# Edge keys by a TensorE matmul per job into PSUM, in place of a round trip through DRAM

## The chip, the cores and the metric

One core of a Trainium2 chip runs the whole program. TensorE (PE in the profile) multiplies matrices and writes only to PSUM; VectorE (DVE), ScalarE (ACT) and GpSimd (POOL) do the rest; SyncE (SP) issues transfers. The metric is the device time of one execution in microseconds (us), median of three.

## The reference, cut to what matters

A layer of a graph transformer over 384 nodes of width 1024: a layer norm, a graph attention with a mask made from 12288 edges, a mixer beside it, and after both a feed-forward part with one of eight experts. The change touches only the making of the mask:

```python
def _build_mask(edge_index, edge_type, edge_type_weights, dtype):
    src, dst = (edge_index[0], edge_index[1])
    w = jax.nn.softplus(edge_type_weights)
    mask = jnp.full((N, N), -jnp.inf, dtype=dtype)
    mask = mask.at[src, dst].set(w[edge_type - 1])
...
q = x @ wq.T + bq
k = x @ wk.T + bk
v = x @ wv.T + bv
q2 = (q @ wiq.T + biq).reshape(N, H, D).transpose(1, 0, 2)
...
scores = jnp.einsum('hnd,hmd->hnm', q2, k2) * scale + mask[None]
attn = jax.nn.softmax(scores, axis=-1)
```

An edge has the key `src * 384 + dst`. Where the same pair occurs more than once, the last edge counts, so the kernel has to find, among 128 edges that it scatters together, those that a later one overrides.

## The kernel before, in words

All products are made in float32r with each operand split in a high and a low part: high by high, low by high, high by low. **Column jobs** (`column_job`, L1143 to L1157) make 128 output columns of a projection: 8 matmuls with `w_hi` and the high input, 8 with `w_hi` and the low input (both L1151), 8 with `w_lo` (L1156), each 128x384 into one PSUM bank. The first stage is `FIRST` = 32 of them: q, k, v and the inner q, 8 each, into banks 0, 1, 6 and 7 in turn (`A_BANKS`). Row blocks of 18 matmuls of 128x512 follow (L1161, banks 2 to 7), with one column job between them, and then eight pairs of heads: scores (L1242), transposes (L1252), the product with v (L1262), and four column jobs each. The output projections and the feed-forward part end the program.

Weights come in 512 KB transfers on SP's queue (`load_weights`, L321) into slots. ACT rounds a slot to `w_hi` (L463), DVE subtracts to get `w_lo` (L789). In the first stage both run three jobs ahead of PE (`DEPTH` = 3). ACT then writes the high part of a job's result (L523) and DVE the low part (L856), the latter only for the first 24 jobs.

**The edges** are handled beside this, three columns of 128 edges in each of the 32 jobs. DVE casts the ends of the edges (L799), makes the keys as rows `erow` of a 96x128 tile (L802), and POOL stores them in `key_dram` (L413). SP then loads, for each job, 384 keys spread over all 128 partitions into one of two halves of `key_row` (L342), behind three waits: for `key_out`, for `xt_done`, and for the job two before it (`where_ready`); each stands on SP's queue ahead of the load of a later job's weights. In `job(a)` of DVE the three scans of L841 compare the spread keys with the key of the edge in each partition (`ekey`, a column), under the triangle `tri`, and sum up the matches in `dup`; L848 makes the table address `where` from it. POOL scatters each column of edges into one of four tables in DRAM (L422), 96 scatters, and loads the tables back (L431). DVE merges them into `mask` (L864, L866) between the splits of the row blocks, ahead of the first scores.

The order on each engine is that of the program text; semaphores alone tie them. `where_ready` starts at 2 and goes up by one with each job's L848. `xt_done` tells that the input is split; `v_copied` and `score_read` stand ahead of the scores and of the second column job of a pair.

Of the kernel before, what the change touches and what calls it, by code (L numbers as in the profile page):

```python
# [15 lines left out]
F32 = mybir.dt.float32  # L16
F32R = mybir.dt.float32r
I32 = mybir.dt.int32
U32 = mybir.dt.uint32
ALU = mybir.AluOpType  # L20
# [4 lines left out]
P = 128  # L25
N = 384
D = 1024
NT = N // P
# [4 lines left out]
CH = E // P  # L33
CJ = 3
STEPS = CH // CJ
# [12 lines left out]
FIRST = 32  # L48
# [3 lines left out]
A_USES = [(A_SLOTS[a % 4], a // 4) for a in range(FIRST)]  # L52
# [39 lines left out]
LN_BANKS = ((6, 4, 2), (6, 4, 0))  # L92


C_ID, C_TRI, C_ONES, C_EIDX, C_ONE, C_ALL = 0, 128, 256, 384, 392, 520


def gps_layer(nc, x, out, weights, conv, down, upT, up_b, down_b, conv_b, disc, bias_cols,
              rows, edge_weights, edge_rows, edge_cols, consts):
    with ExitStack() as ctx:  # L100
# [3 lines left out]
        def sem(name):  # L104
            return ctx.enter_context(nc.semaphore(name))

        key_dram = nc.dram_tensor("key_dram", [CH, P], F32, kind="Internal").ap()
        tables = [nc.dram_tensor(f"table{g}", [N * N, 1], F32, kind="Internal").ap() for g in range(STREAMS)]


# [12 lines left out]
        U = sb("U", [P, 6 * D], F32)  # L123
        x_rows = U[:, 0:NT * D].rearrange("p (t d) -> p t d", t=NT)
        xn_rows = U[:, NT * D:2 * NT * D].rearrange("p (t d) -> p t d", t=NT)
        key_row = U[:, 3456:3456 + 2 * CJ * P].rearrange("p (s n) -> p s n", s=2)
        key_junk = U[:, 4224:4352]
        later = [U[:, g * NT * N:(g + 1) * NT * N].rearrange("p (t n) -> p t n", t=NT) for g in range(STREAMS - 1)]
        present = U[:, 4608:4608 + NT * N].rearrange("p (t n) -> p t n", t=NT)
# [11 lines left out]
        vs = sb("vs", [P, NT, 2, P], F32R)  # L141
# [3 lines left out]
        cst = sb("cst", [P, C_ALL], F32)  # L145
# [7 lines left out]
        ew_t = sb("ew_t", [P, 8], F32)  # L153

        v2f = V2[:].rearrange("p k n -> p (k n)")
        erow_i = v2f[0:CH, 0:2 * P].bitcast(I32)
        erow = v2f[0:CH, 2 * P:4 * P]
        ecol_i = v2f[:, 4 * P:4 * P + 3 * CH].bitcast(I32)
        v2_rows = v2f.rearrange("p (t d) -> p t d", t=NT)
        ecol = v2f[:, 1536:1536 + 3 * CH]  # L160
# [54 lines left out]
        ew_in = sem("ew_in")  # L215
        edges_in = sem("edges_in")
        x_in = [[sem(f"x_in{t}{c}") for c in range(2)] for t in range(NT)]
        key_out = sem("key_out")
        key_calc = sem("key_calc")
        key_in = [sem(f"key_in{s}") for s in range(2)]  # L220
        prep = sem("prep")
        aprep = sem("aprep")
        norm_step = sem("norm_step")
# [92 lines left out]
        @block.sync  # L316
        def _(sp):
            def load_weights(slot, use, src):

                sp.wait_ge(lo_ready[slot], use + 1)  # L320
                sp.dma_start(raw[slot][:], src).then_inc(w_in[slot], 16)  # L321

            for t in (0, 2):
                sp.dma_start(x_rows[:, t, 0:HALF], x[t * P:(t + 1) * P, 0:HALF]).then_inc(x_in[t][0], 16)
            load_weights(*A_USES[0], weights[0])
            sp.dma_start(ew[:], edge_weights.partition_broadcast(P)).then_inc(ew_in, 16)
            sp.dma_start(cst[:, C_TRI:C_ALL], consts[:, C_TRI:C_ALL]).then_inc(cst_in, 16)
            load_weights(*A_USES[1], weights[1])
            sp.dma_start(erow_i, edge_rows).then_inc(edges_in, 16)
            sp.dma_start(ecol_i, edge_cols).then_inc(edges_in, 16)  # L330
            sp.dma_start(bias[:], bias_cols).then_inc(const_in, 16)
            sp.dma_start(disc_in[:], disc).then_inc(const_in, 16)
            load_weights(*A_USES[2], weights[2])
            for a in range(3, FIRST + 2):
                if a < FIRST:
                    load_weights(*A_USES[a], weights[a])
                k, s = a - 3, (a - 3) % 2

                sp.wait_ge(key_out, 16)
                sp.wait_ge(xt_done, NT)  # L340
                sp.wait_ge(where_ready, k + 1)
                sp.dma_start(key_row[:, s, :],  # L342
                             key_dram[k * CJ:k * CJ + CJ, :].rearrange("c e -> (c e)").partition_broadcast(P)
                             ).then_inc(key_in[s], 16)
            sp.wait_ge(where_ready, FIRST)
            sp.dma_start(key_row[:, 1, :],
                         key_dram[(FIRST - 1) * CJ:FIRST * CJ, :].rearrange("c e -> (c e)").partition_broadcast(P)
                         ).then_inc(key_in[1], 16)
            for r in range(JOBS):
                load_weights(*slot_use(r), weights[32 + r])  # L350
            for b in range(16):
                load_weights(*C_USES[b], weights[72 + b])
                if b == 5:

                    sp.wait_ge(vs_ready, KB)
                if b == 7:

                    sp.wait_ge(score_read, KB * 6 + 1)
                if 5 <= b < 9:
                    load_weights(*E_USES[(b - 5)], weights[72 + 16 + (b - 5)])  # L360
            for e in range(4, 8):
                load_weights(*E_USES[e], weights[72 + 16 + e])

            sp.wait_ge(x2_turned, NT)
            sp.dma_start(bias_rows[0:1, :], rows[2:3, :]).then_inc(base_in, 16)

            sp.wait_ge(idx_ready, 1)
            expert = sp.value_load(pick_i[0:1, 0:1], min_val=0, max_val=EXPERTS - 1)
            sp.dma_start(raw_down, down[ds(expert, 1)].rearrange("a p k r -> (a p) k r")).then_inc(small_in, 16)
            sp.dma_start(raw_up, upT[ds(expert, 1)].rearrange("a p k r -> (a p) k r")).then_inc(small_in, 16)  # L370
            sp.dma_start(raw_upb, up_b[ds(expert, 1)].rearrange("a p k -> (a p) k")).then_inc(small_in, 16)
            sp.dma_start(raw_downb[0:R, :], down_b[ds(expert, 1)].rearrange("a r o -> (a r) o")).then_inc(small_in, 16)
            sp.dma_start(bias_rows[1:2, :], conv_b[ds(expert, 1)]).then_inc(convb_in, 16)
            for b, (s, use) in enumerate(V_USES):
                load_weights(s, use, conv[ds(expert * 8 + b, 1)].rearrange("a p n -> (a p) n"))
            for half in range(2):
                c = slice(half * HALF, (half + 1) * HALF)
                for t in range(NT):
                    sp.wait_ge(y_ready, half * NT + t + 1)
                    sp.dma_start(out[t * P:(t + 1) * P, c], x_rows[:, t, c]).then_inc(stored, 16)  # L380
            sp.wait_ge(stored, 16 * 2 * NT)
# [3 lines left out]
        def _(pool):  # L385
# [13 lines left out]
                (mixv_ready, 1), (mix_ready, 1), (o_summed, 1)] + [(b, 1) for b in bank_free]  # L399
            for n, (s, k) in enumerate(given):  # L400
                pool.memset(tiny[:, n:n + 1], 0.0).then_inc(s, k)
            pool.memset(Q2[:, 0:2 * NT, :], ABSENT).then_inc(blanked, 1)

            pool.wait_ge(blanked, 1)
# [3 lines left out]
            for g in range(1, STREAMS):  # L408
                pool.dma_start(tables[g].rearrange("(t p n) o -> p t (n o)", t=NT, p=P),
                               blank[1]).then_inc(scattered[g], 16)  # L410

            pool.wait_ge(key_calc, 1)
            pool.dma_start(key_dram, erow[:, 0:P]).then_inc(key_out, 16)  # L413

            pool.wait_ge(blank_ready, 3)
            pool.dma_start(tables[0].rearrange("(t p n) o -> p t (n o)", t=NT, p=P),
# [298 lines left out]
        def _(dve):  # L715
# [76 lines left out]
            for t in range(NT):  # L792
# [3 lines left out]
                                  ALU.subtract).then_inc(xt_done, 1)  # L796
            split_weights(*A_USES[0])
            dve.wait_ge(edges_in, 32)
            dve.tensor_copy(erow, erow_i).then_inc(prep, 1)  # L799
            dve.tensor_copy(ecol[:], ecol_i).then_inc(prep, 1)  # L800
            dve.wait_ge(prep, 5)
            dve.scalar_tensor_tensor(out=erow[:, 0:P], in0=erow[:, 0:P], scalar=float(N), in1=erow[:, P:2 * P],  # L802
                                     op0=ALU.mult, op1=ALU.add).then_inc(key_calc, 1)
            split_weights(*A_USES[1])


# [4 lines left out]
            src_c, dst_c, type_c = (ecol[:, c * CH:(c + 1) * CH] for c in range(3))  # L811
            dve.scalar_tensor_tensor(out=ekey[:], in0=src_c, scalar=float(N), in1=dst_c,
                                     op0=ALU.mult, op1=ALU.add).then_inc(prep, 1)
            dve.wait_ge(prep, 7)
            dve.wait_ge(id_in, 16)
            dve.wait_ge(cst_in, 16)
            dve.tensor_scalar(diag_w, ident, ew[:, 3:4], None, ALU.mult).then_inc(prep, 1)
# [16 lines left out]

            def job(a):
                m, j, s, ch0 = a // KB, a % KB, a % 2, a * CJ
                dve.wait_ge(key_in[s], (a // 2) * 16 + 16)
                for c in range(CJ):
                    if c:
                        dve.wait_ge(dup_ready, ch0 + c)  # L840
                    dve.scalar_tensor_tensor(  # L841
                        out=key_junk, in0=key_row[:, s, c * P:(c + 1) * P],
                        scalar=ekey[:, ch0 + c:ch0 + c + 1], in1=tri, op0=ALU.is_equal, op1=ALU.mult,
                        accum_out=dup[:, ch0 + c:ch0 + c + 1]).then_inc(dup_ready, 1)
                dve.wait_ge(dup_ready, ch0 + CJ)
# [289 lines left out]
        def _(pe):  # L1135
# [72 lines left out]
            pe.wait_ge(cst_in, 16)  # L1208
            pe.wait_ge(xt_hi, NT + 1)

            for a in range(FIRST):
                pe.wait_ge(bank_free[a % 4], a // 4 + 1)
                column_job(*A_USES[a], T0 if a >= 3 * KB else xT, A_BANKS[a % 4], (xt_done, NT) if a == 0 else None)

            for half in range(2):
                for kp in range(4):
                    row_block(*slot_use(V2_JOBS[half][kp]), T2, [PS[:, b, :] for b in V2_BANKS[half]], kp,
                              kp == 0, kp == 3)
                if half == 0:

                    for s in range(4):
                        pe.wait_ge(bank_free[s], 1 + FIRST // 4)
                    column_job(*slot_use(K2_FIRST), T1, 0)
# [242 lines left out]
```

## Time and profile before

| what | us |
|---|---|
| median of 3 runs | 493.94 |
| lowest and highest run | 493.63, 496.20 |
| the profiled execution's own time | 493.71 |
| its span, first to last instruction | 491.9 |

The profile is one execution. Its span is 1.8 us shorter than that execution's own time, which is 0.2 us under the median. Of the span PE is busy for 481.7 us, DVE for 348.7, ACT for 243.5 and POOL for 123.2; the granted TensorE clock is full in every slice. A matmul's duration in the rows overlaps that of the next, so a stream's cost is read from its length divided by its count.

### The profile page before, as it was taken

What the parts mean: (1) busy time and instruction counts of PE and PEld (TensorE: products, weight loads), DVE (VectorE), ACT (ScalarE), POOL (GpSimd) and SP (SyncE); (2) the same over time, 40 slices, a digit from 0 to 9 for tenths busy, and PEclk for the clock granted to TensorE, in tenths of its full rate; (3) what the DMA queues carried; (4) which work ended last, traced back from release to release, by engine and by line L of the source; (5) the groups of instructions that cost most, each with busy time, mean ns of one, the idle gap of its engine ahead of it and who ended that gap; (6) DMA issues with size and microseconds to landing.
All of it is one profiled execution on the core that took longest, in us unless ns stands there. A gap on an engine that the chain in (4) does not pass through costs nothing.

```text
span 491.9 us, 7479 instructions
## 1 busy us (share of the span) xinstructions
PE 481.7 (98%) x2674; PEld 448.1 (91%) x2674; DVE 348.7 (71%) x845; ACT 243.5 (49%) x421; POOL 123.2 (25%) x145
## 2 busy tenths in 40 slices
PE   6899999999999999999999999999999999999996
PEld 5899999999998888999999999999998888888885
DVE  5888866667544339787869696878776793487295
ACT  2834433333332426675758576676754452154170
POOL 5136677777767800000000000000000000040100
PEclk9999999999999999999999999999999999999999
DMA  7687766656444462322232322225237834301363
GB/s 270 236 277 232 212 189 167 189 167 165 135 162 165 133 232 90 125 87 87 87 114 83 104 86 87 92 80 185 73 130 257 303 123 138 119 1 44 126 260 128
DMA packets 27513, 73.05 MB, mean 148 GB/s; under 512 B 6242, under 2 KB 10946, under 8 KB 27348
## 3 DMA queue, kind: packets, MB, share of 16 engines
q1 hardware_dynamic: 22084, 64.01, 39.0%
q0 software_dynamic: 4960, 7.97, 4.9%
q10 hardware_dynamic: 432, 0.59, 0.4%
q8 instruction: 21, 0.34, 0.3%
q14 instruction: 16, 0.13, 0.1%
HBM read 68.52 MB, written 4.03 MB: 147 GB/s over the span
## 4 chain that ended last, share of the span: by engine, by line
PE 95%; DVE 2%; DMA 1%; issue 1%; ACT 0%; POOL 0%; DVEq 0%; POOLq 0%
PE PS L1151 37%; PE PS L1161 27%; PE PS L1156 18%; PE PS L1262 3%; PE PS L1252 3%; PE PS L1242 3%; PE PS L1390 1%; DMA U<-x 1%; PE PS L1139 1%; PE PS L1394 1%; DVE U L1127 1%; PE PS L1374 1%; DVE stats L760 0%; PE PS L1271 0%; PE PS L1269 0%
## 5 line engine op out<-in xcount | busy, mean ns | idle before, releaser
L789 DVE TENSOR_TENSOR w_lo<-raw,w_hi 128x1024 fp32r<-128x1024 f32 x86 | 104.6, 1219 | 45.1 <-ACT w_hi L463 44.9
L463 ACT ACTIVATE w_hi<-raw 128x1024 fp32r<-128x1024 f32 x87 | 92.0, 1058 | 73.2 <-PE PS L1161 52.1
L422 POOL DMA_INDIRECT table<-evalue,where x96 | 102.7, 1070 | 43.5 <-issue 26.1
L1151 PE MATMUL PS<-xT_hi,w_hi 128*128 128x384 f32 x336 | 66.8, 340 | 1.3 <-issue 1.3
L1151 PE MATMUL PS<-xT_lo,w_hi 128*128 128x384 f32 x336 | 65.1, 334 | 0.0
L1156 PE MATMUL PS<-xT_hi,w_lo 128*128 128x384 f32 x336 | 65.0, 334 | 0.0
L1151 PEld LDWEIGHTS PS<-xT_hi,w_hi 128*128 128x128 f32 x336 | 58.0, 188 | 2.1 <-issue 2.1
L1151 PEld LDWEIGHTS PS<-xT_lo,w_hi 128*128 128x128 f32 x336 | 58.8, 188 | 0.2 <-DVE xT_lo L795 0.2
L1156 PEld LDWEIGHTS PS<-xT_hi,w_lo 128*128 128x128 f32 x336 | 58.8, 188 | 0.0
L434 POOL DMA_DIRECT2D Q<-rows x1 | 0.5, 547 | 165.2 <-DVE q_lo L894 165.2
L1161 PE MATMUL PS<-w_hi,T_hi 128*128 128x512 f32 x144 | 39.3, 391 | 0.0
L1161 PE MATMUL PS<-w_hi,T_lo 128*128 128x512 f32 x144 | 39.0, 389 | 0.0
L841 DVE SCALAR_TENSOR_TENSOR U<-U,V,cst 128x128 f32<-128x128 f32 x96 | 33.5, 349 | 5.7 <-DMA U<-key_dram 3.3
L1161 PE MATMUL PS<-w_lo,T_hi 128*128 128x512 f32 x144 | 37.5, 389 | 0.0
L523 ACT ACTIVATE T_hi<-PS,bias 128x384 fp32r<-128x384 f32 x24 | 13.9, 578 | 44.8 <-PE PS L1156 44.8
L1161 PEld LDWEIGHTS PS<-w_hi,T_lo 128*128 128x128 f32 x144 | 27.0, 188 | 5.7
L1161 PEld LDWEIGHTS PS<-w_lo,T_hi 128*128 128x128 f32 x144 | 27.0, 188 | 5.6
L1161 PEld LDWEIGHTS PS<-w_hi,T_hi 128*128 128x128 f32 x144 | 26.9, 188 | 5.3
L575 ACT ACTIVATE U<-U,nmax 128x384 f32<-128x384 f32 x48 | 28.9, 606 | 1.9 <-DVE nmax L938 1.7
L934 DVE CUSTOM_DVE_ANT_0 U<-PS,mask 128x384 f32<-128x384 f32 x48 | 24.9, 552 | 6.7 <-issue 6.7
L856 DVE SCALAR_TENSOR_TENSOR T_lo<-PS,bias,T_hi 128x384 fp32r<-128x384 f32 x24 | 14.7, 614 | 17.0 <-ACT T_hi L523 17.0
L951 DVE TENSOR_TENSOR probT_lo<-PS,probT_hi 128x384 fp32r<-128x384 f32 x48 | 23.6, 542 | 0.1
(233 smaller groups left out, 796.3 us busy)
## 6 DMA issues: line engine op xcount, KB each, us to landing
raw<-weights SPq DMA_DIRECT2D x84, 512.0 KB, 3.3
U<-key_dram SPq DMA_DIRECT2D x32, 192.0 KB
mask<-weights SPq DMA_DIRECT2D x9, 512.0 KB, 5.4
table<-Q POOLq DMA_DIRECT2D x4, 576.0 KB
V<-conv SPq DMA_DIRECT2D x4, 512.0 KB, 5.4
U<-table POOLq DMA_DIRECT2D x3, 576.0 KB, 8.1
table<-evalue,where POOLq DMA_INDIRECT x96
U<-x POOLq DMA_DIRECT2D x1, 1536.0 KB, 7.6
```

The source lines that it names most:

```text
L422: pool.indirect_dma_start(tables[k % STREAMS], bass.IndirectOffsetOnAxis(ap=where[:, k:k + 1], axis=0), evalue[:, k:k + 1], None, bounds_c ...
L463: act.activation(w_hi[slot][:], raw[slot][:], ACT.Copy).then_inc(hi_ready[slot], 1)
L575: act.activation(prob[:, h, t, :], prob[:, h, t, :], ACT.Exp, bias=nmax[:, h, t:t + 1], scale=SCALE, accum_out=ssum[:, h, t:t + 1]).then_i ...
L789: dve.tensor_tensor(w_lo[slot][:], raw[slot][:], w_hi[slot][:].bitcast(F32), ALU.subtract).then_inc(lo_ready[slot], 1)
L841: dve.scalar_tensor_tensor(out=key_junk, in0=key_row[:, s, c * P:(c + 1) * P], scalar=ekey[:, ch0 + c:ch0 + c + 1], in1=tri, op0=ALU.is_eq ...
L934: dve.tensor_tensor_reduce(prob[:, h, t, :], PS[:, score_bank(j, h, t), 0:N], mask[:, t, :], 1.0, 3.0 * ABSENT, ALU.add, ALU.max, smax[:, ...
L951: dve.tensor_tensor(probT[1][:, t, :], PS[:, TURN_BANKS[h][t], 0:N], probT[0][:, t, :].bitcast(F32), ALU.subtract).then_inc(pT_ready, 1)
L1151: pe.matmul(o, w_hi[slot][:, k * P:(k + 1) * P], src[part][:, k, :], start=(k == 0 and part == 0), stop=False)
L1156: last = pe.matmul(o, wl, src[0][:, k, :], start=False, stop=(k == KB - 1))
L1161: return pe.matmul(bank, src[part][:, 2 * kp + k2, t * P:(t + 1) * P], weights_in[slot][:, k2 * HALF:(k2 + 1) * HALF], start=start, stop=stop)
L1242: last = pe.matmul(PS[:, score_bank(j, h, t), 0:N], q_part[qc][own, t * P:(t + 1) * P], k_part[kc][own, :], start=(n == 0), stop=(n == 2))
L1252: last = pe.transpose(PS[:, TURN_BANKS[h][m], t * P:(t + 1) * P], prob[:, h, t, m * P:(m + 1) * P], ident)
```

## The change

The keys are made and spread by TensorE. The ends of the edges are laid out on the host as 64 rows of 384: row `k` the sources of job `k`, row `32 + k` the destinations. DVE casts them into `ends` (in the tile `vs`, which is used only later), and copies a constant 128x32 tile `pick` whose column `k` has 384 in row `k` and 1 in row `32 + k`. POOL zeroes the other 64 rows of `ends`. One matmul with column `a` of `pick`, read 128 times over as the stationary side, and `ends` as the moving side gives `384 * src + dst` for the 384 edges of job `a` on all 128 partitions, in one of the banks 2 to 5. `key_dram`, its store, the 32 loads of `key_row` and L802 are gone.

```diff
+KEY_BANKS = (2, 3, 4, 5)
...
-            for a in range(3, FIRST + 2):
-                if a < FIRST:
-                    load_weights(*A_USES[a], weights[a])
-                k, s = a - 3, (a - 3) % 2
-
-                sp.wait_ge(key_out, 16)
-                sp.wait_ge(xt_done, NT)
-                sp.wait_ge(where_ready, k + 1)
-                sp.dma_start(key_row[:, s, :],
-                             key_dram[k * CJ:k * CJ + CJ, :].rearrange("c e -> (c e)").partition_broadcast(P)
-                             ).then_inc(key_in[s], 16)
...
+            for a in range(3, FIRST):
+                load_weights(*A_USES[a], weights[a])
...
+            pool.wait_ge(bank_free[-1], 1)
+            pool.memset(ends[2 * STEPS:P, :].bitcast(F32), 0.0).then_inc(ends_zero, 1)
+            pool.wait_ge(ends_zero, 1)
             pool.memset(Q2[:, 0:2 * NT, :], ABSENT).then_inc(blanked, 1)
...
-            pool.wait_ge(key_calc, 1)
-            pool.dma_start(key_dram, erow[:, 0:P]).then_inc(key_out, 16)
...
             dve.wait_ge(edges_in, 32)
-            dve.tensor_copy(erow, erow_i).then_inc(prep, 1)
-            dve.tensor_copy(ecol[:], ecol_i).then_inc(prep, 1)
-            dve.wait_ge(prep, 5)
-            dve.scalar_tensor_tensor(out=erow[:, 0:P], in0=erow[:, 0:P], scalar=float(N), in1=erow[:, P:2 * P],
-                                     op0=ALU.mult, op1=ALU.add).then_inc(key_calc, 1)
+            dve.tensor_copy(ends[0:2 * STEPS, :], erow_i).then_inc(ends_ready, 1)
+            dve.wait_ge(cst_in, 16)
+            dve.tensor_copy(pick, cst[:, C_PICK:C_ALL]).then_inc(ends_ready, 1)
+            dve.tensor_copy(ecol[:], ecol_i).then_inc(prep, 2)
...
-                dve.wait_ge(key_in[s], (a // 2) * 16 + 16)
+                dve.wait_ge(key_done, a + 1)
...
-                        out=key_junk, in0=key_row[:, s, c * P:(c + 1) * P],
+                        out=key_junk, in0=PS[:, KEY_BANKS[a % 4], c * P:(c + 1) * P],
...
+            def keys(a):
+
+                if a >= 4:
+                    pe.wait_ge(where_ready, 2 + a - 3)
+                pe.matmul(PS[:, KEY_BANKS[a % 4], 0:CJ * P], pick[:, a:a + 1].broadcast_to([P, P]), ends,
+                          start=True, stop=True).then_inc(key_done, 1)
+
             for a in range(FIRST):
+                if a == 1:
+                    pe.wait_ge(ends_zero, 1)
+                    pe.wait_ge(ends_ready, 2)
+                    keys(0)
+                    keys(1)
+                if 0 < a < FIRST - 1:
+                    keys(a + 1)
                 pe.wait_ge(bank_free[a % 4], a // 4 + 1)
                 column_job(*A_USES[a], T0 if a >= 3 * KB else xT, A_BANKS[a % 4], (xt_done, NT) if a == 0 else None)
 
+            pe.wait_ge(where_ready, 2 + FIRST)
```

PE's queue at the start of the first stage, before; the third job's rows (`hi_ready2`) follow at once on the second's:

```order
L1156 MATMUL PS<-xT_hi,w_lo 128x384 x7
L1151 MATMUL PS<-xT_hi,w_hi 128x384 [waits hi_ready1,bank_free1]
L1151 MATMUL PS<-xT_hi,w_hi 128x384 x7
L1151 MATMUL PS<-xT_lo,w_hi 128x384 x8
L1156 MATMUL PS<-xT_hi,w_lo 128x384 [waits lo_ready1]
L1156 MATMUL PS<-xT_hi,w_lo 128x384 x7
L1151 MATMUL PS<-xT_hi,w_hi 128x384 [waits hi_ready2,bank_free2]
```

The same place now, where L1202 is the matmul of `keys` (`vs` is the tile that holds `pick` and `ends`), L1138 and L1143 are the lines of the column job:

```order
L1143 MATMUL PS<-xT_hi,w_lo 128x384 x7
L1202 MATMUL PS<-vs 128x384 [waits ends_ready,ends_zero]
L1202 MATMUL PS<-vs 128x384 x2
L1138 MATMUL PS<-xT_hi,w_hi 128x384 [waits hi_ready1,bank_free1]
L1138 MATMUL PS<-xT_hi,w_hi 128x384 x7
L1138 MATMUL PS<-xT_lo,w_hi 128x384 x8
L1143 MATMUL PS<-xT_hi,w_lo 128x384 [waits lo_ready1]
L1143 MATMUL PS<-xT_hi,w_lo 128x384 x7
L1202 MATMUL PS<-vs 128x384
L1138 MATMUL PS<-xT_hi,w_hi 128x384 [waits hi_ready2,bank_free2]
```

Three key matmuls now stand ahead of the second job and one ahead of each later one, up to the thirty-first; from the fifth on they wait for `where_ready`.

SP's queue at the same time, before:

```order
L321 DMA mask<-weights 128x1024 [waits lo_ready6]
L342 DMA U<-key_dram 128x384 [waits where_ready,xt_done,key_out]
L321 DMA raw<-weights 128x1024 [waits lo_ready0]
L342 DMA U<-key_dram 128x384 [waits where_ready,xt_done,key_out]
L321 DMA raw<-weights 128x1024 [waits lo_ready1]
```

And now:

```order
L322 DMA mask<-weights 128x1024 [waits lo_ready6]
L322 DMA raw<-weights 128x1024 [waits lo_ready0]
L322 DMA raw<-weights 128x1024 [waits lo_ready1]
L322 DMA raw<-weights 128x1024 [waits lo_ready2]
```

The weight loads stand behind the split of their slot alone.

## Rows read from the trace of the kernel before

**Rows 1.** The page: PE's busy share, granted clock by slice, chain by engine and line.
```profile
PE 481.7 (98%) x2674; PEld 448.1 (91%) x2674; DVE 348.7 (71%) x845; ACT 243.5 (49%) x421; POOL 123.2 (25%) x145
...
PEclk9999999999999999999999999999999999999999
...
PE 95%; DVE 2%; DMA 1%; issue 1%; ACT 0%; POOL 0%; DVEq 0%; POOLq 0%
```

**Rows 2.** Everything PE waited for: engine, line, releaser, us, times, longest.
```profile
PE PS L1139 <- DVE U L777: 2.6, 1, 2.6
PE PS L1198 <- DVE w_lo L756: 1.6, 1, 1.6
PE PS L1151 <- issue: 1.3, 1, 1.3
PE PS L1242 <- ACT V L535: 0.8, 1, 0.8
```

**Rows 3.** The chain in order of time: start, us, what; first stage to second pair.
```profile
16.84 3.24 PE PS L1151 x16
...
25.62 2.77 PE PS L1151 x16
...
146.26 2.77 PE PS L1151 x16
...
150.42 16.36 PE PS L1161 x72
...
187.37 0.61 ACT V L535
...
188.11 1.86 PE PS L1242 x18
...
194.34 3.04 PE PS L1151 x16
...
199.75 2.77 PE PS L1151 x16
...
211.54 1.77 PE PS L1242 x18
...
217.67 2.77 PE PS L1151 x16
```

**Rows 4.** Busy time by engine from job 2 to job 30; (x) is the instructions begun.
```profile
core 0: us, PE busy (x) PEld busy (x) DVE busy (x) ACT busy (x) POOL busy (x), PEclk, DMA share, GB/s
25.62:146.26 120.64, 120.64 (x698) 120.64 (x697) 84.13 (x266) 45.86 (x60) 84.13 (x79) 1.00 0.64 192
```

**Rows 5.** Two lines' matmuls: ns min/median/max, first and last start; shapes.
```profile
L1151 PE MATMUL PS<-xT_hi,w_hi x336: 331/334/443, 16.8 to 362.7; 128*128 128x384 f32 x168
...
L1156 PE MATMUL PS<-xT_hi,w_lo x336: 334/334/336, 19.9 to 365.4; 128*128 128x384 f32 x168
```

**Rows 6.** The timeline of DVE as the edges begin: start, us, what, idle before.
```profile
19.41 0.28 DVE L799 CAST V<-V 96x256 f32<-96x256 int32 x1
...
27.40 0.35 DVE L841 SCALAR_TENSOR_TENSOR U<-U,V,cst 128x128 f32<-128x128 f32 x1 [1.13 <-DMA U<-key_dram]
```

**Rows 7.** The timeline of DVE in job 12, whose matmuls start at 67.06.
```profile
67.88 0.62 DVE L856 SCALAR_TENSOR_TENSOR T_lo<-PS,bias,T_hi 128x384 fp32r<-128x384 f32 x1 [1.16 <-ACT T_hi L523]
...
68.41 0.34 DVE L841 SCALAR_TENSOR_TENSOR U<-U,V,cst 128x128 f32<-128x128 f32 x1
...
69.59 0.16 DVE L848 SCALAR_TENSOR_TENSOR where<-V 128x3 int32<-128x3 f32 x1
```

**Rows 8.** The timeline of ACT and DVE at the end of the first stage.
```profile
143.82 1.06 ACT L463 ACTIVATE w_hi<-raw 128x1024 fp32r<-128x1024 f32 x1 [5.26 <-DMA raw<-weights]
...
149.64 0.16 DVE L848 SCALAR_TENSOR_TENSOR where<-V 128x3 int32<-128x3 f32 x1
```

**Rows 9.** L422 on POOL in 50 us; the timeline of DVE at merge and scores.
```profile
50.00:100.00 50.00, 37.12 (x36) 1.00 0.68 188
...
181.65 0.76 DVE L864 TENSOR_SCALAR U<-U 128x1152 f32<-128x1152 f32 x1 [7.74 <-DMA U<-table]
...
191.05 0.55 DVE L934 CUSTOM_DVE_ANT_0 U<-PS,mask 128x384 f32<-128x384 f32 x1
```

More of the change, by code:

```diff
@@ L92 @@
 LN_BANKS = ((6, 4, 2), (6, 4, 0))
-C_ID, C_TRI, C_ONES, C_EIDX, C_ONE, C_ALL = 0, 128, 256, 384, 392, 520
+C_ID, C_TRI, C_ONES, C_EIDX, C_ONE, C_PICK, C_ALL = 0, 128, 256, 384, 392, 520, 552
+KEY_BANKS = (2, 3, 4, 5)
 def gps_layer(nc, x, out, weights, conv, down, upT, up_b, down_b, conv_b, disc, bias_cols,
@@ L105, in sem @@
             return ctx.enter_context(nc.semaphore(name))
-        key_dram = nc.dram_tensor("key_dram", [CH, P], F32, kind="Internal").ap()
         tables = [nc.dram_tensor(f"table{g}", [N * N, 1], F32, kind="Internal").ap() for g in range(STREAMS)]
@@ L125, in gps_layer @@
         xn_rows = U[:, NT * D:2 * NT * D].rearrange("p (t d) -> p t d", t=NT)
-        key_row = U[:, 3456:3456 + 2 * CJ * P].rearrange("p (s n) -> p s n", s=2)
         key_junk = U[:, 4224:4352]
@@ L155, in gps_layer @@
         v2f = V2[:].rearrange("p k n -> p (k n)")
-        erow_i = v2f[0:CH, 0:2 * P].bitcast(I32)
-        erow = v2f[0:CH, 2 * P:4 * P]
+        erow_i = v2f[0:2 * STEPS, 0:CJ * P].bitcast(I32)
+        vs_flat = vs[:].rearrange("p t h d -> p (t h d)")
+        ends = vs_flat[:, 0:CJ * P]
+        pick = vs_flat[:, CJ * P:CJ * P + STEPS]
         ecol_i = v2f[:, 4 * P:4 * P + 3 * CH].bitcast(I32)
@@ L217, in gps_layer @@
         x_in = [[sem(f"x_in{t}{c}") for c in range(2)] for t in range(NT)]
-        key_out = sem("key_out")
-        key_calc = sem("key_calc")
-        key_in = [sem(f"key_in{s}") for s in range(2)]
+        ends_zero = sem("ends_zero")
+        ends_ready = sem("ends_ready")
+        key_done = sem("key_done")
         prep = sem("prep")
@@ L333, in _ @@
             load_weights(*A_USES[2], weights[2])
-            for a in range(3, FIRST + 2):
-                if a < FIRST:
-                    load_weights(*A_USES[a], weights[a])
-                k, s = a - 3, (a - 3) % 2
-                sp.wait_ge(key_out, 16)
-                sp.wait_ge(xt_done, NT)
-                sp.wait_ge(where_ready, k + 1)
-                sp.dma_start(key_row[:, s, :],
-                             key_dram[k * CJ:k * CJ + CJ, :].rearrange("c e -> (c e)").partition_broadcast(P)
-                             ).then_inc(key_in[s], 16)
[L345 to L348, printed above, removed]
+            for a in range(3, FIRST):
+                load_weights(*A_USES[a], weights[a])
             for r in range(JOBS):
@@ L813, in _ @@
                                      op0=ALU.mult, op1=ALU.add).then_inc(prep, 1)
-            dve.wait_ge(prep, 7)
+            dve.wait_ge(prep, 8)
             dve.wait_ge(id_in, 16)
@@ L1440 @@
     consts[:, C_ONE:C_ONE + P] = 1.0
+    for k in range(STEPS):
+        consts[k, C_PICK + k] = N
+        consts[STEPS + k, C_PICK + k] = 1.0
     arrays = {
@@ L1453 @@
         "edge_weights": a["gnn_edge_type_weights"],
-        "edge_rows": np.concatenate(edges[:2], axis=1),
+        "edge_rows": np.concatenate([e.reshape(STEPS, CJ * P) for e in edges[:2]]),
         "edge_cols": np.concatenate([e.T for e in edges], axis=1),
```

## The prediction

> **What bounds the kernel now.** I read the page first: PE is busy for 98% of the span at full granted clock, and 95% of the chain that ended last is PE's [rows 1]. That says that the bound is TensorE, but not that it is TensorE in the stretch that the change touches, so the list of PE's own waits comes next. It has four entries in the whole program [rows 2]: two while the input is normalised, one of 1.3 us before the first column job, and 0.8 us before the first scores, where ACT empties the last bank of the row blocks. None names a key, a scan, a split or a weight transfer.
>
> The chain in order of time then shows the first stage as one unbroken row of matmuls [rows 3]. Job 2 starts at 25.62 and job 31 at 146.26. That is 29 jobs of 24 matmuls in 120.64 us: 4.160 us for a job and **173.3 ns for a matmul** of 128x384. The window over the same stretch confirms it from the other side: PE busy for 120.64 of 120.64 us with 698 matmuls begun, against the 696 of the 29 jobs, while DVE is busy for 84.13, POOL for 84.13 and ACT for 45.86 [rows 4]. The single matmul's duration of 334 ns [rows 5] is not its cost: two are in flight at a time, so the pitch counts.
>
> So the transfers of keys, and DVE's waits for them (1.13 us before the very first scan [rows 6]), lie beside a stream that never waited for them.
>
> **The change part by part.**
>
> *What is removed.* 32 loads of 192 KB, one store, one small DVE operation, and on SP's queue three waits ahead of each weight load. DVE gains its waits for keys, SP its freedom, the transfer engines 6 MB. The cover over all of it is the PE stream, which is full without it, so each counts 0 us. Below nothing it could count only by letting PE run faster; that is a rival below.
>
> *What is added on PE.* 32 key matmuls with 384 moving columns, full height and width, in float32r like their neighbours: the shape of the rows that surround them. PE has no idle time in the stage to hide them in [rows 4]. At the pitch of the stage that is 32 x 173.3 ns = **5.55 us**, all of it on the path. The trace has no matmul with one weight column repeated 128 times, nor one alone in its bank between two jobs, so I bound a key matmul from both sides. Cheapest: the score matmuls, 384 columns but only 64 rows high, run at 18 in 1.77 us [rows 3], 98 ns each; 32 of them would be 3.1 us. A key matmul is 128 rows high, as those at 173 ns are, so it should not get there. Dearest: one that shares nothing with its neighbours costs its whole duration of 334 ns [rows 5]; 32 would be 10.7 us. I take 173.3, since each job in the stage already begins with a matmul that waits on semaphores and opens a new bank, and 29 such starts have left no gap in 120.64 us.
>
> The trace puts 384 columns at 173.3 ns, also where no keys are loaded: from 199.75 to the end of its row, 16 such matmuls take 2.77 us [rows 3]. The Trainium skill, on the page "TensorE: Matmul & The Clock Gate", section "Back-to-back issue gap", gives N / 2.4 + 2.5 ns for a warm matmul, 162.5 ns here; by that, 32 would be 5.2 us in place of 5.55. The row disagrees with the rule by 11 ns, and the sum goes by the row.
>
> *The waits added on PE.* A wait on PE holds everything behind it, that is the whole column job, so each must be met early. The first waits for DVE's casts. They now come at the place of L799, which starts at 19.41 and takes 0.28 us for 256 columns [rows 6]; with 384 columns and a further 32 they should be done by about 20.0, and PE gets there when job 0 is over, 4.3 to 4.6 us after 16.84 [rows 3], so after 21.1. One microsecond of slack: 0 us. POOL's zeros come in its first 6 us or so. From the fifth key matmul on, `keys(a + 1)` ahead of job `a` waits for job `a - 3`'s table address. In job 12, whose matmuls start at 67.06, L848 starts at 69.59 [rows 7], 2.5 us into its job; so the awaited one is 3 x 4.16 - 2.7 = 9.8 us old when PE asks. 0 us. The wait at the end of the stage is for the last L848. Before, it began at 149.64 [rows 8] with the stage ending at 150.42 [rows 3], a slack of only 0.6 us. But it was late for a reason that goes: ACT's rounding of the first slot of the row blocks stood idle for 5.26 us for its weights [rows 8], as their load stood behind the last key loads on SP. With the loads free, this rounding can start when job 28's matmuls are over, and the last address should come about 4 us before PE wants it. 0 us.
>
> *What moves on DVE.* The scans read the keys from PSUM and no longer from SBUF. L856 reads 384 columns of PSUM in 0.62 us and L841 128 columns of SBUF in 0.34 us [rows 7]: 256 columns more for 0.28 us, or 1.1 ns a column, which leaves about 0.2 us of fixed cost in either. So PSUM brings next to nothing; were it 0.1 us for each scan, it would be 0.3 us a job against the 4.16 - 84.13 / 29 = 1.26 us that DVE has free in each job [rows 4]. The lows of the weights stay on time: 0 us on the path.
>
> *What is late next.* DVE merges the tables just ahead of the first scores. The first table arrives at 181.65, and DVE reads the first scores at 191.05 [rows 9], though they were there some 2 us before (scores start at 188.11 [rows 3]). PE feels it once: the second column job of that pair takes 3.04 us for its first 16 matmuls where the next pair's takes 2.77 [rows 3], a stall of **0.27 us**. The scatters run at 36 in 50 us [rows 9], three in 4.17 us, the pace of PE's jobs. They get slower with these, by up to 24 x 0.17 = 4.2 us over the jobs in which DVE also evacuates, while PE comes 5.55 us later. The merge so gains at least 1.3 us on the scores, and the stall goes: -0.27 us. Its other end is 0, if POOL is delayed in full.
>
> *The sum.* 5.55 - 0.27 = **5.28 us**. On the profiled execution that is 493.71 + 5.28 = 498.99. The median of the runs is 493.94, 0.2 us above the profiled one, so I expect **499.2 us**.
>
> **The rivals.**
>
> *A key matmul does not pipeline with its neighbours* (its repeated column loads more slowly, or its wait keeps the next weights from being loaded ahead). Against it stand the job starts that cost nothing; for it, that no row shows such an operand. Fully unpipelined it is 10.7 - 0.27 = 10.4 us: 504.4. Half way it is about 501.8.
>
> *PE waits for DVE*, at the start (casts), or at the end of the stage (last address). The slacks are 1 us and about 4 us. If the weights of the row blocks came no earlier than before in relation to PE, the scans at 0.1 us more each would just use up the old 0.6 us. With 1 to 2 us lost it is 500.2 to 501.2.
>
> *Faster than before.* The mechanism: the matmuls of the stage run at 173.3 ns and not at the 160 ns that 384 columns take at 2.4 GHz because transfers and scans read and write SBUF beside them. Key loads write 192 KB into it in every job. If their going brought the pitch to 160 ns, 32 x 24 matmuls gain 768 x 13.3 ns = 10.2 us, and the key matmuls cost 5.1: 493.9 - 5.1 - 0.3 = 488.5. It is faster from a gain of 7.2 ns a matmul on. Against it: the pitch is the same 173.3 ns at 199.75, where no keys move [rows 3].
>
> *No change that can be measured.* It needs half of the cost covered. If the key matmuls ran at the 98 ns of the scores, it is 3.1 - 0.3 = 2.8 us, 496.8, still at the edge. Or DVE's earlier merge helps the pairs by more than the one stall that the chain shows; I find no second one.
>
> **How the numbers follow.** What a measurement can tell here is about 0.5%, 2.5 us. Chances: the forecast of 173 ns each, 0.77; dearer key matmuls, 0.09; PE waits for DVE, 0.05; a cost of half or less, 0.06; faster, 0.03. The range takes in the forecast without its small gain and with a job start or two that stumble, the waits on DVE and the half-way case of the dear matmul: up to 502.0. Downwards it takes the rule's price and a run of the spread seen, to 497.6. This leaves out the full price at the top, the cheap and the faster case at the bottom, some 0.15. Slower by over 0.5%, that is above 496.4: 0.90; within: 0.07; faster: 0.03.
>
> **What would show it.** In the profile after: about 32 matmuls of a new line, each 173 ns after the one before; jobs 2 to 30 in 125.5 us from start to start of the first and last, PE busy throughout; row blocks starting 5.5 us later; no wait of PE for a cast, for L848's successor or for a bank; the second column job of the first pair at 2.77 and not 3.04; DVE's wait for tables down by over a microsecond. A gap after each key matmul would point to the first rival, one at a single place to the second, and a pitch under 173 ns within the column jobs to the faster case.

## The result and the profile after

The changed kernel takes 500.0 us (median of six runs, 499.52 to 500.23), the one before 493.79 us: a ratio over the runs of 1.0113, with a 95% interval of 1.0096 to 1.0130 (the two medians alone give 1.0126). One of the six runs of the kernel before took 501.03 us, the others 493.45 to 496.20. The change is slower by 6.2 us. The forecast was 5.3 us slower, 499.2; the time lies in its range of 497.6 to 502.0. The profiled execution took 500.23 us with a span of 498.4, against 493.71 and 491.9 before: 6.5 us more in either.

The page of the changed kernel, as in [rows 1]: PE's busy share, its granted clock, the chain.

```profile
PE 489.4 (98%) x2706; PEld 455.7 (91%) x2706; DVE 349.3 (70%) x845; ACT 243.2 (49%) x421; POOL 128.8 (26%) x145
...
PEclk9999999999999999999999999999999999999999
...
PE 95%; DVE 2%; DMA 1%; issue 1%; ACT 0%; POOL 0%; DVEq 0%; POOLq 0%
```

Everything that PE waited for in it, as in [rows 2]:

```profile
PE PS L1185 <- DVE w_lo L744: 1.6, 1, 1.6
PE PS L1126 <- DVE U L765: 1.4, 1, 1.4
PE PS L1138 <- issue: 1.3, 1, 1.3
PE PS L1244 <- ACT V L523: 0.8, 1, 0.8
```

The same four entries; the first of [rows 2], while the input is normalised, is 1.2 us shorter here. None of the new waits on PE (casts, zeros, table addresses, four banks) cost anything. PE has 32 instructions more and 7.7 us more busy time: the 6.5 us of the span and those 1.2 us. The chain in order of time (start, us, what), to be held against [rows 3]; L1202 is the key matmul, L1138 and L1143 the column job, L1148 the row blocks, L1244 the scores:

```profile
16.92 3.24 PE PS L1138 x16
...
34.97 0.17 PE PS L1202
35.15 2.78 PE PS L1138 x16
...
56.73 0.18 PE PS L1202
56.90 2.80 PE PS L1138 x16
...
148.60 2.80 PE PS L1138 x16
...
156.95 16.36 PE PS L1148 x72
...
194.63 1.86 PE PS L1244 x18
...
200.85 2.77 PE PS L1138 x16
```

The first stage, from the first column job to the row blocks, is 156.95 - 16.92 = 140.03 us against 150.42 - 16.84 = 133.58 before: **6.45 us more**, practically the whole difference. The row blocks are unchanged (16.36), and the second column job of the first pair has its 0.27 us back, 2.77 for 3.04. A job in the middle of the stage takes (148.60 - 56.90) / 21 = 4.367 us against 4.160, so a key matmul costs 207 ns there and not 173. Its own row is short (0.17 or 0.18); the other 30 ns stand in the row behind it, 2.80 us for the first 16 matmuls of the next job where [rows 3] have 2.77. Early in the stage, at 35 us, it is 2.78, and a job takes 4.34.

The window from job 2 to the start of job 31, as in [rows 4] (columns as there), shows how little the rest matters:

```profile
26.44:152.79 126.35, 126.35 (x726) 126.35 (x725) 87.03 (x281) 44.46 (x59) 98.20 (x87) 1.00 0.39 127
```

The transfers' share fell from 0.64 to 0.39 and their rate from 192 to 127 GB/s, and no matmul became faster.

### The profile page after: what moved, and what is told of

It reads as the page before. It is cut to its first block, busy times and chain, and to the rows that moved or that the text cites. A ratio compares the mean times of both kernels' runs of the same rounds, so it can differ in the third digit from the quotient of the medians.

```text
span 498.4 us, 7482 instructions
## 1 busy us (share of the span) xinstructions
PE 489.4 (98%) x2706; PEld 455.7 (91%) x2706; DVE 349.3 (70%) x845; ACT 243.2 (49%) x421; POOL 128.8 (26%) x145
## 4 chain that ended last, share of the span: by engine, by line
PE 95%; DVE 2%; DMA 1%; issue 1%; ACT 0%; POOL 0%; DVEq 0%; POOLq 0%
PE PS L1138 36%; PE PS L1148 26%; PE PS L1143 18%; PE PS L1254 3%; PE PS L1264 3%; PE PS L1244 3%; PE PS L1392 1%; DMA U<-x 1%; PE PS L1126 1%; PE PS L1202 1%; PE PS L1396 1%; DVE U L1114 1%; PE PS L1376 1%; DVE stats L748 0%; PE PS L1271 0%
## 5 line engine op out<-in xcount | busy, mean ns | idle before, releaser
L410 POOL DMA_INDIRECT table<-evalue,where x96 | 108.4, 1129 | 33.6 <-issue 22.6
L1138 PE MATMUL PS<-xT_hi,w_hi 128*128 128x384 f32 x336 | 67.4, 342 | 1.3 <-issue 1.3
L1143 PE MATMUL PS<-xT_hi,w_lo 128*128 128x384 f32 x336 | 65.1, 334 | 0.0
L1138 PE MATMUL PS<-xT_lo,w_hi 128*128 128x384 f32 x336 | 65.1, 334 | 0.0
L1138 PEld LDWEIGHTS PS<-xT_hi,w_hi 128*128 128x128 f32 x336 | 58.6, 188 | 1.8 <-issue 1.8
L1138 PEld LDWEIGHTS PS<-xT_lo,w_hi 128*128 128x128 f32 x336 | 58.9, 188 | 0.3 <-DVE xT_lo L783 0.3
L1143 PEld LDWEIGHTS PS<-xT_hi,w_lo 128*128 128x128 f32 x336 | 58.8, 188 | 0.0
L422 POOL DMA_DIRECT2D Q<-rows x1 | 0.5, 549 | 174.1 <-DVE q_lo L881 174.1
L1148 PE MATMUL PS<-w_hi,T_hi 128*128 128x512 f32 x144 | 39.3, 391 | 0.0
L1148 PE MATMUL PS<-w_hi,T_lo 128*128 128x512 f32 x144 | 39.0, 389 | 0.0
L1148 PE MATMUL PS<-w_lo,T_hi 128*128 128x512 f32 x144 | 37.5, 389 | 0.0
L828 DVE SCALAR_TENSOR_TENSOR U<-PS,V,cst 128x128 f32<-128x128 f32 x96 | 33.5, 349 | 2.3
L1148 PEld LDWEIGHTS PS<-w_hi,T_lo 128*128 128x128 f32 x144 | 27.0, 188 | 5.7
L1148 PEld LDWEIGHTS PS<-w_lo,T_hi 128*128 128x128 f32 x144 | 27.0, 188 | 5.6
L1148 PEld LDWEIGHTS PS<-w_hi,T_hi 128*128 128x128 f32 x144 | 26.9, 188 | 5.3
```

The costliest lines, as they stand in the source:

```text
L410: pool.indirect_dma_start(tables[k % STREAMS], bass.IndirectOffsetOnAxis(ap=where[:, k:k + 1], axis=0), evalue[:, k:k + 1], None, bounds_c ...
L828: dve.scalar_tensor_tensor(out=key_junk, in0=PS[:, KEY_BANKS[a % 4], c * P:(c + 1) * P], scalar=ekey[:, ch0 + c:ch0 + c + 1], in1=tri, op0 ...
L1138: pe.matmul(o, w_hi[slot][:, k * P:(k + 1) * P], src[part][:, k, :], start=(k == 0 and part == 0), stop=False)
L1143: last = pe.matmul(o, wl, src[0][:, k, :], start=False, stop=(k == KB - 1))
L1148: return pe.matmul(bank, src[part][:, 2 * kp + k2, t * P:(t + 1) * P], weights_in[slot][:, k2 * HALF:(k2 + 1) * HALF], start=start, stop=stop)
```

## The experiments

All numbers of a job are from start to start in the chain or the trace. In the traces of the first four runs and of `e9_even_tile`, `e10_batches`, `e11_quad` and `e12_quad_again` PE stands still again and again without waiting for anything that the trace names; in `e1_four` it does so in eight pieces of up to 1.4 us between 54.6 and 63.6. The kernel before took 519.34, 516.39 and 514.78 us beside them, in place of 494. So their whole times say little, and I read job lengths in stretches without such an interruption.

The question was where the 33 ns beyond 173 come from. The candidates: the place between two jobs; the scans, which now read PSUM while PE writes there; the wait at the key matmul; its increment, right behind that of the job's last matmul; the repeated column as the stationary side.

**Only four key matmuls.**

```diff
-                dve.wait_ge(key_done, a + 1)
+                dve.wait_ge(key_done, min(a + 1, 4))
...
-                if 0 < a < FIRST - 1:
+                if 0 < a < 3:
                     keys(a + 1)
```

> The changed kernel with the key matmuls of the first 4 jobs alone; the other 28 are left out, all scans read those 4 banks, and the table addresses are fixed numbers, so the mask is not the reference's. Nothing else moves. Theory (the key matmuls are the whole cost, 173 ns each and some 30 ns in the job behind them): job 2 to 30 at 4.160 us each again, first stage 134.3 us long against 133.58 before and 140.03 changed, whole kernel about 494.3. Rival (DVE's scans reading PSUM beside PE's writes slow the matmuls): jobs stay at 4.19, stage 135.2. If the forecast's second term holds, the second column job of the first pair still has its 0.27 us back.

Chain of `e1_four`, jobs without a key matmul:

```profile
34.77 2.77 PE PS L1138 x16
37.54 1.39 PE PS L1143 x8
38.93 2.77 PE PS L1138 x16
```

4.16 us for a job, with DVE scanning PSUM all along and without any transfer of keys. So the scans and the freed transfers together change nothing, and the key matmuls are the whole cost of the stage. That a cost of the scans and a gain from the transfers cancel is not excluded by this run; against it stands that [rows 3] have the same pitch at 199.75, where no keys move. The whole time, 522.93 us beside 519.34 for the kernel before (ratio 1.011, 0.989 to 1.033), could not confirm the 494.3.

**Every key matmul twice.**

```diff
-                pe.matmul(PS[:, KEY_BANKS[a % 4], 0:CJ * P], pick[:, a:a + 1].broadcast_to([P, P]), ends,
-                          start=True, stop=True).then_inc(key_done, 1)
+                for n in range(2):
+                    last = pe.matmul(PS[:, KEY_BANKS[a % 4], 0:CJ * P], pick[:, a:a + 1].broadcast_to([P, P]), ends,
+                                     start=True, stop=True)
+                last.then_inc(key_done, 1)
```

> The changed kernel with every key matmul issued twice into the same bank, the increment on the second. If the 30 ns beyond 173 belong to the place (one interruption between two jobs, however long), 32 further matmuls cost 173 ns each: first stage 140.03 + 5.55 = 145.6 us, whole kernel 505.6. If they belong to the operand (the repeated column of pick, or ends), 206 ns each: 146.6 us, whole kernel 506.6.

Chain of `e2_double`:

```profile
35.72 0.35 PE PS L1203 x2
36.06 2.77 PE PS L1138 x16
...
40.23 0.35 PE PS L1203 x2
```

Neither outcome. A job takes 4.513 us, so two key matmuls cost 353 ns together, only 6 beyond 2 x 173.3: the extra went, it neither stayed nor doubled.

**The wait moved ahead.** The wait for the table address ahead of the `w_lo` matmuls of the job before:

```diff
             def keys(a):
 
-                if a >= 4:
-                    pe.wait_ge(where_ready, 2 + a - 3)
...
+                if freed:
+                    pe.wait_ge(where_ready, freed)
                 pe.wait_ge(lo_ready[slot], use + 2)
```

> The changed kernel with the key matmul's wait for the table address moved ahead of the w_lo matmuls of the job before, so that from the fourth key matmul on none waits itself; the same matmuls otherwise. If the wait at the key matmul makes the 30 ns in the job behind it: jobs at 4.333 us in place of 4.366, first stage 139.1 us. If place or operand make them: 140.0 us, unchanged.

Chain of `e3_early_wait`:

```profile
77.65 0.18 PE PS L1202
77.83 2.80 PE PS L1138 x16
...
82.02 0.18 PE PS L1202
```

4.37 us as in the changed kernel, and 4.34 in its early jobs. The wait is not the cause.

**An ordinary matmul in the same place**, in the kernel before:

```diff
+            def extra(a):
+
+                pe.matmul(PS[:, (2, 3, 4, 5)[a % 4], 0:N], xT[0][:, 0, 0:P], xT[0][:, 0, :],
+                          start=True, stop=True)
...
+                if a == 1:
+                    extra(0)
+                    extra(1)
+                if 0 < a < FIRST - 1:
+                    extra(a + 1)
```

> The kernel before, keys by transfers as there, with 32 idle matmuls of 128x384 in the places of the key matmuls: ordinary weights (a slice of the high input) and the high input moving, no wait, no increment, result in banks 2 to 5 read by nobody. If the place alone makes the 30 ns: first stage 140.0 us, jobs 4.366. If the repeated column, the wait, the increment or the scans on PSUM make them: 139.1 us, jobs 4.333. Whole kernel 500 or 499.4, as here the merge gets no help from the freed transfers.

Chain of `e4_plain`:

```profile
39.18 0.17 PE PS L1213
39.35 2.77 PE PS L1151 x16
...
43.51 0.17 PE PS L1213
```

4.333 us: exactly 173.3 ns more than a job of before. The place costs nothing. This is the prediction's price, and it is right for a matmul with an ordinary stationary side.

**The same with an increment, and the same with a repeated column.** `e5_plain_inc` and `e8_plain_wide` change one thing each in `e4_plain`:

```diff
-                          start=True, stop=True)
+                          start=True, stop=True).then_inc(extra_done, 1)
```

> The kernel before with the 32 idle matmuls of e4_plain, each of which now also increments a semaphore that nobody waits for. In e4_plain a job with such a matmul took 4.333 us, with the key matmul 4.367. If the increment, right behind that of the job's last matmul, makes the 33 ns: 4.367. If operand or readers make them: 4.333.

```diff
-                pe.matmul(PS[:, (2, 3, 4, 5)[a % 4], 0:N], xT[0][:, 0, 0:P], xT[0][:, 0, :],
+                pe.matmul(PS[:, (2, 3, 4, 5)[a % 4], 0:N], xT[0][:, 0, 0:1].broadcast_to([P, P]), xT[0][:, 0, :],
```

> The kernel before with the 32 idle matmuls of e4_plain, without increment, their stationary side now one column of the high input read 128 times over, as pick is. If the repeated column makes the 33 ns: jobs at 4.367 us. If not: 4.333.

Chain of `e5_plain_inc`, then of `e8_plain_wide`:

```profile
56.53 0.17 PE PS L1214
56.70 2.77 PE PS L1152 x16
...
156.03 16.36 PE PS L1162 x72
```

```profile
56.85 0.18 PE PS L1213
57.02 2.80 PE PS L1151 x16
...
157.07 16.36 PE PS L1161 x72
```

The stage starts at 16.89 and 16.93 in them. It is 139.14 us long with the increment, jobs of 4.333, and **140.14 us with the repeated column, jobs of 4.367**, as in the changed kernel. Whole: 499.13 and 500.15 us, one run each, beside 494.01 for the kernel before. So the repeated column alone brings the surcharge, with other data, without a wait, an increment, a reader or any of the change's other parts. In `e8_plain_wide` all jobs from the second on have it, the early ones too; why four early jobs of the changed kernel (4.34) nearly escape it is open.

**128 equal columns that are really there.** `e9_even_tile` gives the idle matmul a tile of ones:

```diff
+        even = vs[:, 0, 0, :]
...
+            pool.memset(even.bitcast(F32), 1.0).then_inc(even_in, 1)
...
-                pe.matmul(PS[:, (2, 3, 4, 5)[a % 4], 0:N], xT[0][:, 0, 0:P], xT[0][:, 0, :],
+                pe.matmul(PS[:, (2, 3, 4, 5)[a % 4], 0:N], even, xT[0][:, 0, :],
```

> The kernel before with the 32 idle matmuls of e4_plain, their stationary side now a real tile of 128 columns that all hold 1.0. With an ordinary slice a job took 4.333 us, with one column read 128 times over 4.367. If the access pattern (the same address 128 times) makes the 33 ns: 4.333 here. If 128 equal columns make them, however they are stored: 4.367.

Chain of `e9_even_tile`:

```profile
57.91 0.17 PE PS L1218
58.08 2.77 PE PS L1156 x16
...
62.24 0.17 PE PS L1218
```

Jobs of 4.333 us. So it is the access pattern, one address read 128 times, and not equal weights. Other patterns, such as a stride of two, were not tried.

**The key matmuls in the middle of a job**, between its high and its low input:

```diff
-                if 0 < a < FIRST - 1:
-                    keys(a + 1)
+                if a == 1:
+                    keys(2)
...
+                    if part and between:
+                        between()
```

> The changed kernel with the key matmuls from the fourth on moved into the job, between the 8 matmuls with the high input and the 8 with the low one, operand, wait and increment as they are. If two increments on neighbouring matmuls make the 33 ns: jobs at 4.333 us, first stage about 139.0. If operand or readers make them: 4.367 us, 140.0.

Chain of `e7_mid`:

```profile
58.21 1.41 PE PS L1140 x8
...
156.87 16.36 PE PS L1150 x72
```

The 8 matmuls behind the key matmul take 1.41 us, others 1.39. Jobs of 4.367 us, 4.34 in the early ones, the stage 156.87 - 16.84 = 140.03 us, the whole 499.85. This is the outcome for the operand; where the matmul stands makes no difference.

**Two by two.**

```diff
-                if 0 < a < FIRST - 1:
-                    keys(a + 1)
+                if a == 1:
+                    keys(2)
+                if a > 1 and a % 2:
+                    keys(a)
+                    if a < FIRST - 1:
+                        keys(a + 1)
```

> The changed kernel with the key matmuls two by two, ahead of every second job from the third on; the same matmuls, waits and increments. In e2_double two that read the same column cost 353 ns together, 6 beyond 2 x 173.3. If that holds for two different columns: 2 jobs in 8.67 us in place of 8.73, first stage 139.2 us, whole kernel 499.4. If each change of the repeated column costs its 33 ns: 8.73 us, 140.0, 500.

Chain of `e10_batches`:

```profile
38.86 2.77 PE PS L1138 x16
...
47.19 0.34 PE PS L1202 x2
47.53 2.80 PE PS L1138 x16
```

Two jobs in 47.53 - 38.86 = 8.67 us, later 8.674 on average: 354 ns for two different repeated columns, 7 beyond the plain price. The surcharge belongs to a single such matmul among others and is nearly gone for two in a row. It stands in single rows behind a batch, as in the last row above.

**The 33 ns are two parts.** The starts of the single matmuls in the traces show them. Behind the key matmul at 56.56 in the changed kernel they are 177, 175, 178, 185, 176 and 181 ns apart, in place of 173: some 6 ns at once, then some 27 over the next four. Behind the four key matmuls that nearly escape (30.5 to 43.5) and behind most pairs there is only the first part, 6 to 7 ns. And the second part is not peculiar to the repeated column. The kernel before has none, and yet the column job behind its first row blocks starts with 175, 177, 185, 176 and 182 ns:

```profile
166.78 2.80 PE PS L1151 x16
```

`e4_plain` has the same steps once, behind an interruption at 118 us. So the repeated column itself costs 6 to 7 ns, and in most jobs it sets off a further 27 that other disturbances of the stream set off too. What decides whether they follow is open.

**Two keys side by side in 64 rows each**, which tests the lower bound of 98 ns:

```diff
+                own = slice(64 * (a % 2), 64 * (a % 2) + 64)
+                pe.matmul(PS[:, KEY_BANKS[a % 4], 0:CJ * P], pick[own, a:a + 1].broadcast_to([64, P]), ends[own, :],
+                          start=True, stop=True).then_inc(key_done, 1)
```

> A version of the change: the ends laid out twice, in rows 0 to 63 and 64 to 127, so that a key matmul needs 64 rows only, and two of them, on the two halves and into two banks, stand together ahead of every second job; POOL's zeroing is gone. If they run as the scores of the kernel before do, 98 ns each (the lower bound of the prediction), 16 pairs cost 16 x 0.20 = 3.1 us: 2 jobs in 8.52 us in place of 8.73, first stage 136.8 us, whole kernel 496.9. If they run one after the other: 140 us or a little less, whole kernel as changed, 500.

Chain and timeline (start, us, engine, line, shape) of `e6_half`:

```profile
55.52 2.77 PE PS L1134 x16
...
59.69 0.37 PE PS L1199 x2
60.06 2.98 PE PS L1134 x16
...
64.42 1.73 PE PS L1134 x10
...
59.62 0.44 PE L1199 MATMUL PS<-vs 64*128 64x384 f32 x2
59.99 0.62 PE L1134 MATMUL PS<-xT_hi,w_hi 128*128 128x384 f32 x2
```

Slower, not faster: 503.54 us, ratio 1.0167 (1.0096 to 1.0238). Of its four runs two took 502.4. The profiled one, 505.03, begins the first stage 2.6 us later than the changed kernel (19.48), with a granted clock of 0.77 from 12 us on up to there and before any key matmul; its stage of 142.24 us is 8.7 longer than before, which fits 502.4. Two jobs take 64.42 - 55.52 = 8.90 us, 0.58 above 8.32, where two keys of full height cost 0.41. The two do begin 3 ns apart. But from the last matmul of the job ahead to the pair it is 269 ns in place of 173, the pair takes 0.37, and the first matmul behind it 285 ns. PE loses time at the change of height on either side. The 98 ns of the scores hold in a stream of 18. I should have seen it in the chain of before, where the column job behind the scores takes 2.98 us for 16 matmuls and not 2.77:

```profile
213.31 2.98 PE PS L1151 x16
```

**Four side by side in 32 rows each**, ahead of every fourth job:

```diff
-                if 0 < a < FIRST - 1:
-                    keys(a + 1)
+                if a in (1, 5, 8, 12, 16, 20, 24, 28):
+                    for n in range(4):
+                        keys(a // 4 * 4 + n)
```

> A version of the change: the ends of four jobs laid out in four groups of 32 rows, and four key matmuls of 32 rows each, on the four groups and into the four banks, ahead of every fourth job. In e6_half a pair of 64 rows began 3 ns apart and cost 0.58 us in all, most of it before and behind the pair (269 and 285 ns at the changes of height). If four begin together and the changes of height cost the same: 8 x 0.58 = 4.6 us, first stage 138.2 us, whole kernel 498.1, faster than the changed kernel and still slower than the one before. If four begin one after the other, at 370 ns for each: 8 x 1.3 us, 505.

Chain of `e11_quad` (one of the four keys has no record):

```profile
48.02 2.77 PE PS L1134 x16
...
52.19 0.38 PE PS L1199 x3
52.57 2.98 PE PS L1134 x16
...
56.93 2.77 PE PS L1134 x16
```

The job ahead of the batch and the one behind take 56.93 - 48.02 = 8.91 us, 0.59 above 8.32, for four keys and no longer two. That is 0.15 us a key against 0.21 in the changed kernel, 4.7 us for all 32.

> The version of e11_quad once more, on another chip, for its whole time: the stage lengths of e11_quad could be read only where no stall from outside fell into them (a batch of four keys cost 0.58 us there, so 4.65 us for 8). If nothing else changes, the first stage is 138.2 us and the whole kernel 4.65 - 0.25 = 4.4 us above the kernel before, ratio 1.009, and some 2 us under the changed kernel. If the later wait for four free banks holds up DVE or the scatters so that the scores wait, it is as slow as the changed kernel.

The whole time stays open. The ratios to the kernel before were 1.003 (0.998 to 1.008) and 0.997 (0.992 to 1.001), with interruptions in both kernels. By the lengths of the jobs it would be about 4.4 us over the kernel before, a ratio of 1.009, and 2 us under the changed one. Both intervals leave 1.009 out, so the whole times do not bear the estimate out; with single runs from 507 to 521 us they do not settle it either. The wait for four free banks cost nothing in `e11_quad` and 0.7 us once in `e12_quad_again`. No version here has a sum below the kernel before.

## Why the prediction was right, and where it was off

**The bound** was read rightly. This PE stream without a gap takes every added matmul onto the path, and gives nothing for freed transfers: `e1_four` has the old 4.160 us a job with neither.

**The price of a key matmul** is the term that was mis-sized. I took 173.3 ns, from rows around it that were like it in all but the repeated column, and said that no row shows such an operand. An ordinary matmul in that place costs exactly that (`e4_plain`). With the repeated column it is 207 ns in most jobs, so the stage grew by 6.45 and not by 5.55 us, and jobs 2 to 30 took 126.35 us where 125.5 was said. That 5.28 forecast and 6.2 measured lie close owes something to the small size of a surcharge for which the prediction had no row. The bounds of 98 and 334 ns held, but the lower one for the wrong reason: alone between two jobs, the cheap form costs more (`e6_half`). The page's rule for a warm matmul that the prediction weighed, 162.5 ns here by the Trainium skill, page "TensorE: Matmul & The Clock Gate", section "Back-to-back issue gap", is again below every such row, by 11 ns; the section gives it for an isolated matmul and says that in a stream of weight loads and matmuls both set the spacing.

**The waits on PE** cost nothing, as forecast. The casts and the last address of the changed kernel, on the timeline of DVE (start, us, what, idle before), for [rows 6] and [rows 8]:

```profile
19.49 0.34 DVE L787 CAST vs<-V 64x384 fp32r<-64x384 int32 x1
19.76 0.17 DVE L789 CAST vs<-cst 128x32 fp32r<-128x32 f32 x1
...
152.34 0.16 DVE L835 SCALAR_TENSOR_TENSOR where<-V 128x3 int32<-128x3 f32 x1
```

The casts end at 19.93, 1.3 us ahead of the weight load of the first key matmul, which begins at 21.2. The last address begins at 152.34, 4.6 us before the row blocks, where "about 4" was said; ACT no longer waits for the weights of their first slot.

**The scans on PSUM** take 349 ns on average, as on SBUF: nothing added.

**The merge and the scores.** The stall of 0.27 us went, but for another reason than I gave. DVE's timeline, for [rows 9]:

```profile
180.35 0.75 DVE L851 TENSOR_SCALAR U<-U 128x1152 f32<-128x1152 f32 x1
...
195.58 0.56 DVE L921 CUSTOM_DVE_ANT_0 U<-PS,mask 128x384 f32<-128x384 f32 x1
```

I expected the scatters to end later by up to 4.2 us. Their last one begins at 164.8, before at 168.8: 4 us earlier. Of these 3.2 are there from the start, as the first begins at 28.4 in place of 31.6: before, it sat behind a wait of 7.8 us for the transfer that blanks its table, which is gone. The other 0.8 is open. The longer jobs are not the reason: in `e8_plain_wide`, with jobs of 4.367 us and the keys by transfer, the last scatter begins at 171.4, 2.6 us later than before, as I had expected here. So in the changed kernel the merge does not wait for the tables at all, where it waited 7.7 us before. Yet the stall is gone in `e5_plain_inc` and `e8_plain_wide` too (2.77 in their second column job of the first pair), where DVE still waits 5.9 and 4.8 us for a table. It is enough that PE comes later.

**The rest.** From the pairs on PE loses 0.2 us bit by bit, where column jobs behind the transposes take 2.81 us for 16 matmuls and not 2.77; `e7_mid`, the same work in another order, loses nothing there. The starts behind the transposes at 206.0 show the same 178, 185, 176 and 181 ns as those behind a key matmul; what sets them off is open here too. In sum: 6.45 - 0.25 + 0.2 and 0.1 from before the stage, the 6.5 of the span.

**The rivals.** Dearer key matmuls came true in small, by 33 ns each and not by 160, through the repeated column that I had named. PE waiting for DVE, a pitch freed by less traffic, and a cost of half or less did not.

## What to carry to other kernels

Where one engine runs without a gap, expect work that is moved onto it to cost its full pitch, however small the work looks and however much it frees elsewhere; read the pitch from a long stream, and ask which feature of the new instruction no row shows. A trick that is fast in a stream (matmuls of partial height side by side) must be priced with its changes on either side: two in a batch cost 0.29 us each here, four 0.15, a full one 0.21. Here 6 MB of transfers and 32 waits bought nothing, since nothing waited for them.

## What the runs showed of the hardware that was not expected

- A float32r matmul whose stationary side reads one column 128 times makes it and the matmuls behind it 33 ns later in sum in most jobs (4.367 against 4.333 us): 6 to 7 ns at once, and 27 over four later starts (178, 185, 176, 182 ns). A stored tile of 128 equal columns does not, and two such matmuls in a row cost 6 to 7 ns together.
- Those four late starts come without a repeated column too, behind the row blocks of the kernel before (2.80 us for 16 matmuls at 166.78, elsewhere 2.77).
- Matmuls of 64 or 32 rows on different row groups begin 3 to 4 ns apart. Going from 128 rows to them took 268 to 269 ns and back, at the first full matmul, 278 to 285 ns, against 173 in the stream, so a pair as well as a batch of four costs 0.58 to 0.59 us.
- A scan of 128 columns takes 349 ns on average from PSUM as from SBUF, and PE's jobs stay at 4.160 us beside it (`e1_four`).
